# Products with V and scores as whole runs on TensorE in a six-layer windowed-attention kernel

## The reference, cut to what matters

```
for i in range(DEPTH):                       # 6
    x = attn_layer(shift_tokens(x), Wqkv[i], q_scale[i], k_scale[i], Wo[i]) + x
    x = ffn_layer(shift_tokens(x), ln_g[i], ln_b[i], W1[i], b1[i], W2[i], b2[i]) + x

def attn_layer(x, Wqkv, qs, ksc, Wo):
    q, k, v = split(x @ Wqkv)                # 16 heads of 64
    q = l2norm(q) * qs; k = l2norm(k) * ksc  # then rotated by tables (rotary)
    out = local_attention(q, k, v)           # windows of 32, each looks at itself and the one before
    return out @ Wo

def local_attention(q, k, v):
    sim = bq @ bk2 * QK_SCALE                # 32 x 64 per window and head, masked
    return softmax(sim) @ bv2
```

## Time and profile before

| | |
|---|---|
| median of 3 runs | 2149.88 us (2148.3 to 2151.88) |
| span of the profiled execution | 2143.9 us |
| TensorE matmuls busy | 2022.6 us, 94% |
| TensorE weight loads busy | 1356.1 us, 63% |
| VectorE busy | 1497.0 us, 70% |
| ScalarE busy | 1286.6 us, 60% |
| GpSimd busy | 1522.5 us, 71% |
| mean granted clock of TensorE | 0.984 |

### The profile page before, as it was taken

The page is one execution under the profiler, slowest core; times in us unless marked ns, Lnnn a source line. Parts: engine busy times, 40 slices in busy tenths (PEclk is TensorE's granted clock), DMA queues, the critical chain, the costliest instruction groups (busy, mean ns, idle before and its releaser), DMA issues.

```text
span 2143.9 us, 84229 instructions
## 1 busy us (share of the span) xinstructions
PE 2022.6 (94%) x35763; PEld 1356.1 (63%) x35763; DVE 1497.0 (70%) x2268; ACT 1286.6 (60%) x1844; POOL 1522.5 (71%) x2307
## 2 busy tenths in 40 slices
PE   4789999878999999999999999999999999999997
PEld 1455555545666667666766667666676666766675
DVE  2445454458877887777877787777877788778773
ACT  3567777634656665665656565566656666566653
POOL 3344444458878887788877778778887788777880
PEclk8899999998999999999999999999999999999998
DMA  4999999932323222242222422224222242222221
GB/s 125 289 347 355 344 357 344 348 126 61 74 62 111 68 65 65 63 113 67 72 62 62 113 62 69 65 62 120 63 66 62 63 117 70 62 62 63 68 72 43
DMA packets 120004, 261.51 MB, mean 122 GB/s; under 512 B 29092, under 2 KB 34128, under 8 KB 118864
## 3 DMA queue, kind: packets, MB, share of 16 engines
q1 hardware_dynamic: 119632, 256.13, 41.4%
HBM read 87.06 MB, written 68.29 MB: 72 GB/s over the span
## 4 chain that ended last, share of the span: by engine, by line
PE 68%; POOL 4%; DVE 3%; issue 2%; ACT 1%; POOLq 0%; DVEq 0%; ACTq 0%
PE ring L463 22%; PE ring L529 9%; PE ring L473 8%; PE yps L541 7%; PE ring L499 7%; PE ring L569 5%; PE ring L510 4%; PE tpose L579 3%; PE ring L491 1%; POOL roped L275 1%; DVE turned L643 1%; PE tpose L551 1%; DVE ss L652 1%; DVE stats L701 0%; POOL ss L248 0%
## 5 line engine op out<-in xcount | busy, mean ns | idle before, releaser
L643 DVE TENSOR_TENSOR turned<-ring,ropes 128x1024 f32<-128x1024 f32 x384 | 452.0, 1219 | 303.0 <-PE ring L463 303.0
L240 POOL TENSOR_TENSOR roped<-turned 128x512 f32<-128x512 f32 x384 | 522.5, 1386 | 170.4 <-PE ring L473 169.0
L463 PE MATMUL ring<-wqkv,xT 128*128 128x512 f32 x1152 | 567.4, 616 | 5.2 <-ACT xT L328 4.0
L275 POOL TENSOR_TENSOR roped<-roped,rnorm 128x1024 f32<-128x1024 f32 x192 | 361.5, 1904 | 7.5
L1170 POOL TENSOR_SCALAR less<-less,lowest 128x512 f32<-128x512 f32 x256 | 175.3, 697 | 240.0 <-DVE lowest L1139 240.0
L1139 DVE CUSTOM_DVE_ANT_0 less<-ps_b,shifted 128x512 f32<-128x512 f32 x256 | 166.6, 688 | 226.0 <-PE ps_b L1002 79.7
L463 PEld LDWEIGHTS ring<-wqkv,xT 128*128 128x128 f32 x1152 | 198.2, 192 | 161.0 <-issue 149.8
L369 ACT COPY pT<-ring 128x1024 f32<-128x1024 f32 x96 | 97.2, 1012 | 305.8 <-PE ring L510 305.8
L529 PEld LDWEIGHTS ring<-pT,vwin 64*64 64x64 f32 x12288 | 198.5, 134 | 51.9 <-issue 51.5
L317 ACT ACTIVATE squares<-ring 128x1024 f32<-128x1024 f32 x192 | 197.3, 1028 | 55.8 <-DVE turned L643 55.8
L529 PE MATMUL ring<-pT,vwin 64*64 64x32 f32 x12288 | 219.7, 220 | 4.9 <-issue 3.4
(11 more groups left out here) (133 smaller groups left out, 3234.7 us busy)
## 6 DMA issues: line engine op xcount, KB each, us to landing
vwin<-v SPq DMA_DIRECT2D x1536, 64.0 KB, 2.0
shifted<-scratch_w SPq DMA_DIRECT2D x64, 1024.0 KB, 12.6
scratch_w<-wrows SPq DMA_DIRECT2D x48, 1026.0 KB, 10.9
scratch_w<-x SPq DMA_DIRECT2D x16, 1026.0 KB, 10.4
wqkv<-in_l_wqkv SPq DMA_DIRECT2D x6, 1536.0 KB, 6.9
wo<-in_l_wo SPq DMA_DIRECT2D x6, 512.0 KB
w<-in_l_w SPq DMA_DIRECT2D x6, 342.0 KB
w<-in_l_w SPq DMA_DIRECT2D x6, 171.0 KB
```

The lines of the kernel that those rows point to most:

```text
L240: nc.gpsimd.tensor_tensor(halves[2][:, :, side, :], halves[0][:, :, side, :], halves[1][:, :, 1 - side, :], ALU.add).then_inc(s[name + "_a ...
L275: nc.gpsimd.tensor_tensor(whole, whole, norm, ALU.mult).then_inc(s[name + "_roped"], 1)
L463: last = nc.tensor.matmul(out[:, half, :], xT[:, t % SEQT * P:(t % SEQT + 1) * P], wqkv[:, layer_of(t), at + half * 512:at + (half + 1) * ...
L643: ins = nc.vector.tensor_tensor(turned[:, n, part, :].rearrange("p (h d) -> p h d", d=DH), heads, table, ALU.mult)
```

## The change

In TensorE's loop three calls change place: the first half of `attend` goes behind the transposes of k, next to the second half, and the second half of `scores` goes ahead of the projection of Q, next to the first half.

```
                     hidden(g - 2, 2)
-                attend(n - 3, 0)
                 if step == 3:
                     shift(g - 1)
                 if step == 1:
                     project_ffn(g - 2)
                 turn_qk(1, n - 1)
+                attend(n - 3, 0)
                 attend(n - 3, 1)
                 project("V", n)
                 scores(n - 1, 0)
+                scores(n - 1, 1)
                 project("Q", n + 1)
-                scores(n - 1, 1)
                 turn_p(n - 2)
```

## The result

The changed kernel takes 2272.64 us (median of 4 runs, 2268.94 to 2274.64), the kernel before beside it 2149.09 us (4 runs, 2143.15 to 2151.88): ratio 1.0576 [1.0554, 1.0597], slower by 5.8% and outside the predicted range. The profiled execution has a span of 2269.2 us against 2143.9 us, 125.3 us more.

What follows compares the result with a forecast made beforehand. TensorE's own list was taken to bound the kernel. Waits at the transposes of k, less saved switches, gave +2.01 us per group of four periods, +48 us over 24 groups: 2198 us, 2.2% slower, range 2166 to 2225.

Steps and rivals of the forecast that it cites:

- (c): Transposes of k: only the transpose of x now covers the qT copy; reached at K+2.69 in plain periods, startable at K+3.95.
- (d): ScalarE's copy of qT: Q's later place moves its start from K+2.79 to K+3.37, the transposes of k to K+4.53.
- (e): Hidden layers: transposes of k wait for VectorE's gate, starting 6.0 us after the layers do instead of being reached after 5.2.
- (a): Products with V in one run: 2.00 us, saving 0.14 us a period, plus 0.10 in three of four period kinds.
- (b): Scores in one run: priced at 1.68 us, nothing saved inside; 0.14 us a period saved at Q and the transposes of p.
- rival 4: Long runs stop for "issue" (29 us added, 2227) or the clock falls behind waits (20 us, 2218); chance 17%.
- Rival 1: At the transposes of k, copies stay hidden and saved switches win: 34 us faster, 2116; chance 6%.
- Rival 3: A cheaper run of scores, 1.42 us instead of 1.68: 26 us less, 2172; chance 17%.

Runs made afterwards that it cites:

- e10: The kernel before with every matmul of the products with V issued twice, so each half is a run of 128; 2410.92 us, single run.
- e9: e4 with every matmul of the products with V 256 columns wide instead of 32, giving wrong products; 2624.51 us, single run.
- e11: The changed kernel with the first half of the first product with V issued twice, 64 matmuls more, once; 2276.58 us, single run.
- e12: The changed kernel with 32 more matmuls with V, once, moving block ends by a quarter block; 2259.15 us, single run.
- e5: The kernel before with the scores in one run and Q projected ahead of it, products with V in halves; 2137.58 us, ratio 0.9901.
- e8: The kernel before with all products with V ahead of the transposes of k, and Q ahead of one score run; 2184.49 us, ratio 1.0111.
- e4: The changed kernel with the projection of Q ahead of the score run; 2167.97 us, ratio 1.0106 to the kernel before.
- e6: e4 with three of four matmuls of the products with V 64 columns wide instead of 32; 2188.94 us, ratio 1.0154.

## Why the prediction was wrong

**What held.** (c) and (d): the q products at K-2.46 (predicted -2.47), the copy of qT at K+3.28 (+3.37), the transposes of k at K+4.42 (+4.53), idle ahead of them 1.50 us plain (about 1.7) and 0.79 with the shift (about 0.9). (e): the transposes of k 6.25 us behind the hidden layers' start (6.0), idle 0.94 (about 0.8); the profile puts the wait down to ScalarE's gelu and not to VectorE's gate. (a): a run with V that doesn't stop costs 2.00 us, as priced; (b): one of scores 1.71 in that period, and 1.69 in the median of the 63 behind 570 us that don't pause (1.68).

The sum of these held too. I took all periods from K to K, 88 in each kernel, and of each kind the lower quartile as its length without a disturbance:

| kind | before | after | difference | predicted |
|---|---|---|---|---|
| plain | 14.50 | 15.86 | +1.36 | +1.37 |
| shift | 15.65 | 16.29 | +0.64 | +0.60 |
| feed-forward | 17.15 | 16.80 | -0.35 | -0.38 |
| hidden | 19.99 | 20.21 | +0.22 | +0.42 |

That is +1.87 us a group (predicted +2.01), 41 us in these 22 groups. But the 88 periods grew from 1496.6 (574.90 to 2071.52) to 1610.9 us (586.74 to 2197.69), by 114.3. What they have above their lower quartiles grew from 16 to 89 us: 73 us that the sum didn't hold, about what the forecast of 2198 us lacks.

**The step that failed** is the price of a run in (a) and (b), which holds no term for stops: "I price the run at 1.68", and 2.00 for V, are prices of runs that go through. The other score run of the earlier trace rows, which stopped for 1.74 us, was put into rival 4, at one of four of the 96 score runs and 1.2 us, 29 us. The first half of rival 4 is what happened. 26 score runs stopped, about the share that it supposed, but for 1.57 us each (40.8 us by the waits); and 20 runs with V stopped as well (17.4 us), for which nothing was priced. With the 6.5 us of before taken off, that is 52 us more.

Its second half, the lower clock, came on top, but seldom behind the waits from which rival 4 priced it. Between 560 and 2100 us the granted clock is at 0.50, the 1.2 GHz level, in ten stretches, 37.5 us, against two, 6.8 us, before. Eight of the ten begin 0.1 to 1.4 us behind the end of a stop, two behind a wait for qT. At half the clock the difference costs at most (37.5 - 6.8)/2 = 15 us, where all of that time is matmul work. The Trainium skill's page "TensorE: Matmul & The Clock Gate", section "A second HAM failure mode: psum-queue depth-cycling", tells of a clock that oscillates where TensorE idles briefly and often, and the trace agrees in that the fall above stands right behind a stop of 2.02 us. The price of the falls was not tried by itself. With 45 us for the worked-out waits and savings in 24 groups, 52 for the stops and at most 15 for the clock, some 13 us of the 125 are not assigned to a cause.

**Why runs stop** is shown. The instructions come in blocks of 256 (e10), a stop stands at a block's end (all stops of every kernel counted), fewer instructions per us in the runs with V end the stops there (e9), and moving the blocks alone moves the stops (e11, e12). It also goes with the old order being nearly free of them: in halves of 64 a block can't end behind the 64th matmul, and ahead of the 75th only one of the 48 runs that stopped behind 570 us in the changed kernel did so. But a late end isn't enough: of its 75 runs with an end behind the 75th, 47 stopped, and in e5 only 4 of some 37 score runs. Nor is it needed in every order: in e10, with twice the matmuls with V, 15 of the 108 runs with V with an end at the 75th or ahead of it stopped too, and of the halves of before 10 of 181 with an end in them. What sets when a block is asked for, and so which late end finds its block there, stays open; e8 shows that two projections ahead don't decide it alone.

**The other rivals.** Rival 1 needed waits under 1.4 us a group; the two for qT and the gelu alone are about 3 (72 us in 24 groups). Rival 3's cheaper score run exists: the median of the score runs that don't pause is 1.53 us in e4 and in e5 (84 and 88 runs behind 570 us). In the changed kernel a quarter of them cost no more than that, but the median is 1.69. The two projections ahead are not the reason by themselves: e8 has them too, and its median is 1.69 (60 runs). The reason stays open.

## What to carry to other kernels

Count instructions, not only microseconds, where short matmuls are put together: 256 in 2 us were often more than the supply gave, and a projection of 8 instructions in 2 us between two halves was cover for the supply as the half with V was cover for a copy. One stop marked "issue" among two instances of a form that the change will make common is a price to put into the sum, with both kinds of run that will take the form. And before a piece of work is moved, ask what its old place covered: here a copy, a gate, and the next block of instructions.

## What the runs showed of the hardware

- TensorE's instruction stream is cut into blocks of 256, and every stop within a run, 49 in the changed kernel, ends at the same remainder (193 or 194) of the instruction's number; packets of 16 KB end at least 1.1 us ahead of it.
- In the 64x64 form a run of 128 matmuls with three of four 64 columns wide took 2.0 us (e6), as with 32 columns; with 256 columns it took 7.07 us. So up to 64 columns the price is one per matmul, some 15.6 ns.
- The same 128 score matmuls without a pause cost 1.53 us in the median in e4 and e5 and 1.69 in the changed kernel and e8, and single ones from 1.4 to 1.9; no run shows why.
- Eight of the ten falls of TensorE's granted clock to 0.50 in the changed kernel's layers begin within 1.4 us of the end of a stop.
